# Four-layer gated cross-attention and expert block: a re-ordered first stage, its key work moved into the first expert layer, and the zero fill issued from ACT's queue

## The chip, the cores and the metric

One NeuronCore of one Trainium2 chip runs the whole program. The metric is the device time of one execution in microseconds. Each time given for a kernel as a whole is a median over several executions; the trace is of one execution, taken by the hardware profiler.

## The reference, cut to what matters

The input `x` has 8 batches of 128 tokens with 256 features; the context `ctx` has the same shape. Four layers follow one another, each one an attention-like block and an expert block, both added to `x` with a gate:

```python
x = x + tanh(g_xattn[0]) * wkv_recurrence(time_decay, time_first, layernorm(x), ctx)   # layer 0
x = x + tanh(g_ffn[0])   * top2_experts(layernorm(x))        # 8 experts of 176 + a shared one of 352
x = x + tanh(g_xattn[1]) * masked_attention(layernorm(x), ctx)                          # layer 1
x = x + tanh(g_ffn[1])   * top4_experts_with_capacity(layernorm(x))   # 32 experts of 128, 256 seats each
x = x + tanh(g_xattn[2]) * attention_32_heads_rms(layernorm(x), ctx)  # layer 2: k = rmsnorm(ctx @ Wk.T) per head of 8
x = x + tanh(g_ffn[2])   * golden_experts_with_lora(layernorm(x))     # 8 of 256; Wg, Wu, Wd of 2 experts get Ga@Gb etc.
x = x + tanh(g_xattn[3]) * int8_attention(layernorm(x), ctx)          # layer 3: wq, wp rounded to 127 steps per row
x = x + tanh(g_ffn[3])   * top_p_experts(layernorm(x))                # 8 of 512
```

The recurrence of layer 0 keeps three running values per feature (`pp`, `aa`, `bb`): with k = layernorm(x) and v = ctx, `y_t = (e1*aa + e2*v) / (e1*bb + e2)`, where e1, e2, e1b, e2b are exponentials of differences to a running maximum. The kernel computes it by scans over all tokens.

Of layers 2 and 3, some things depend on the context or the weights alone: the keys and values (`ctx @ Wk.T`, `ctx @ Wv.T`), the RMS norm of the keys of layer 2, the weight tiles of the two experts with a low-rank addition, and the rounded `wq`, `wp`. The kernel before computes all of these in its first stage.

## The kernel before, in words

The program is written engine by engine, each with its own ordered list of instructions, and the engines meet only through semaphores. An engine that waits for a semaphore holds up everything behind it in its own list; this is what sets the order of the work. `link(...)` makes an engine wait for its own last instruction. SP only issues DMAs; POOL also issues the indirect ones.

**First stage (about 0 to 119 us).** It does the recurrence of layer 0 and the context work of layers 2 and 3 side by side.

- SP (L422 to L454) loads `x` (one DMA, 1 MB), small vectors, `ctx`, the key and value weights, then `wqp3` and, four times in turn, a weight tile of layer 2 (`fold`, L440) that gets its low-rank addition and is written to DRAM (`folded`, L442). Only then come `wr`, `wq2`, `bq3`, `bp3`, `mask` and the first two weight tiles of the first expert layer (L468).
- PE transposes `ctx` (L1580), then the normalised `x` (`turn(0)`, L1367), then goes through 8 batches `b`: two products of 512 columns (L1635 for layer 2, L1640 and L1641 for layer 3), the transposes of the keys of layer 3 (`turn_k3`, L1611), and after every second `b` the low-rank products (`fold_products`, L1601). After that it turns the rounded weights (L1654, L1658), the recurrence's result (L1668) and the keys of layer 2 (`turn_k2`, L1626).
- ACT copies `ctxT` (L885) and the turned `x` (L863), then per `b` copies and splits the products (L946 to L958), copies `k3T` (L930), and before `b` = 2 and 6 runs the four exponentials of one half of the features (`wkv_exp`, L893). After the loop: a guess of the inverse root by Ln and Exp (L903, L905), the copies `wi`, `wscale`, and the split and copy of each batch of keys (`k2_hi` L916, `k2_out` L936).
- DVE normalises `x` (L2038), then in `wkv()` makes the arguments for both halves `c` (L2052 to L2060, with four minima and maxima each), rounds the weights (`weight_scales`, L2100 to L2112), and per `c` does two scans (L2066, L2068), four products and sums, a reciprocal (L2073) and a product (L2075). Then it scales half of the layer-2 keys (L2271) and adds the recurrence to `x` (`add_banks`, L2085).
- POOL per `b` sums squares for the key norm (L682 to L684) and splits the keys of layer 3 (L687), does the two products of the recurrence (`wkv`, L660), adds the low-rank part (`fold_lora`, L667), scales the diagonals (L673), refines the norms (L694 to L697) and scales and splits the other half of the keys (L703, L711).
- Before the first expert layer, DVE waits for all keys, splits the first weight tile (`gu_lo`, `down_lo`) and normalises `x` again (L2038); PE has `turn(1)` behind it.

**First expert layer, `ffn(0)` (about 119 to 254 us).** 14 tiles of 128 hidden features, each in two halves of 512 tokens. A weight is split in two half-precision parts, so each product is three. For tile `k` PE does `gate_up(k, 0)`, `down(k-1, 0)`, `gate_up(k, 1)`, `down(k-1, 1)` (12 matmuls each, L1406 and L1418). The elementwise chain of one half goes ACT `silu` (L994), DVE `gated` (L2160), POOL `weigh` (L723), ACT `h_hi` (L1020), DVE `h_lo` (L2167). The order within a tile is fixed in both lists:

```python
# ACT: down_hi(k)  silu(k,0)  gu_hi(k+1)  h_hi(k,0)  silu(k,1)  h_hi(k,1)
# DVE: down_lo(k)  gated(k,0) gu_lo(k+1)  h_lo(k,0)  gated(k,1) h_lo(k,1)
```

SP's `loads_0` issues for each tile two broadcast loads of router weights (L499), the weight load (L478) and `clear(i)` (L488): two DMAs per tile that write zeros to the DRAM tables `seats` (8192 rows of 1152 bytes, 9.4 MB) and `slots` (4096 rows of 1024 bytes, 4.2 MB), 28 DMAs in all. POOL waits for all of them (L757) before it scatters tokens into `seats`.

**Layer 1's experts.** After the router, POOL issues 32 indirect DMAs into `seats` (L761, from 304 to 346 us); PE's first transpose of an expert's rows (`expert_turn`, L1532) waits for them and for the loads behind them. DVE meanwhile prepares diagonals (L2404) and splits two weight tiles (L2420).

Of the kernel before, what the change touches and what calls it, by code (L numbers as in the profile page):

```python
# [25 lines left out]
F32 = mybir.dt.float32  # L26
# [8 lines left out]
P = 128  # L35
# [41 lines left out]
def build(nc, a, out):  # L77

    with ExitStack() as ctx:  # L79
# [64 lines left out]
        k_raw = xn  # L144
        k_norm = sb("k_norm", [P, 3, B, H2])
        k_st = sb("k_st", [P, 2, H2, 4, DH2], F16)
        k_sq = k_st[:, 0, :, :, :].rearrange("p h i d -> p (h i d)").bitcast(F32).rearrange("p (k d) -> p k d", k=2)
# [5 lines left out]
        class Arena:  # L153
# [38 lines left out]
        wk_d = ar.take([2, LW])  # L192
        wk_e = ar.take([KD, 4, LW])
        wk_ev = ar.take([2, LW])

        lora = W16[0:LORA_R, :, :, :].rearrange("p a b c -> p (a b c)").bitcast(F32)\
            .rearrange("p (k d) -> p k d", d=D)
        fold = W[:, 0, :]
        fold_add = W[:, 1, :]
        wq_s = sb("wq_s", [P, 3, 4])  # L200
        wq_f = wb[:, 0, :].rearrange("p (w o d) -> p w o d", w=2, o=KD)
        wq_i = wb[:, 1, 0:HALF].bitcast(BF16).rearrange("p (w o d) -> p w o d", w=2, o=KD)
        wq_diag = wb[:, 1, HALF:T].rearrange("p (k o) -> p k o", k=4)
# [42 lines left out]
        m_dest = ar.take([E1, CT]).bitcast(U32)  # L246
        e_x = ar.take([3, CT, ROW])
        e_xT = ar.take([2, 2, KD, CAPACITY], F16)
        e_w16 = ar.take([2, WROW], F16)
        e_y = [ar.take([CT, D]) for _ in range(3)]  # L250
        ar.at = at_back = ARENA - 4 * TOP1 * D
# [71 lines left out]
        KEYS_BEFORE = (2, 6)  # L323

        K2_ORDER = (0, 4, 1, 5, 2, 6, 3, 7)
# [38 lines left out]
        def steps_at(n):  # L364

            return range(max(n - FIRST_UNIT, 0) * 3 // 4, max(n + 1 - FIRST_UNIT, 0) * 3 // 4)

# [53 lines left out]
        def _(sp):  # L421
            sp.dma_start(x[:, :, :], a["x"].rearrange("b s d -> s b d")).then_inc(sem("x_in"), 16)  # L422
# [9 lines left out]
            sp.dma_start(wq_f, a["wqp3"]).then_inc(sem("wqp_in"), 16)  # L432
            for k in range(LORA_T):
                if k:
                    sp.wait_ge(sem("folded_out"), 16 * k)
                if k % (F2 // P) == 0:
                    if k:
                        sp.wait_ge(sem("fold_mm"), k)
                    sp.dma_start(lora[:, :, :], a["lora"][:, k * P // F2]).then_inc(sem("lora_in"), 16)
# [40 lines left out]
            def clear(i):  # L480

                if i == 0:
                    sp.wait_ge(sem("set_up"), SET_UP["zeros"])
# [52 lines left out]
            def loads_1():  # L536
                for k in range(4):
                    expert_weights(k)
# [2357 lines left out]
```

## Time and profile before

| what | value |
|---|---|
| runs without the profiler, median of 3 | 1089.8 us (1087.68 to 1095.57) |
| the profiled execution's own time | 1082.81 us |
| its span, first to last instruction | 1081.0 us |
| mean granted TensorE clock | 0.905 |
| busy share of the span: PE, DVE, ACT, POOL | 80%, 60%, 48%, 35% |

The profiled execution lies 7.0 us under the median of the runs without it. The busy share says how much of the span an engine worked; it is an average over stages with different limits, so each stage is read by itself.

### The profile page before, as it was taken

What the parts mean: (1) busy time and instruction counts of PE and PEld (TensorE: products, weight loads), DVE (VectorE), ACT (ScalarE), POOL (GpSimd) and SP (SyncE); (2) the same over time, 40 slices, a digit from 0 to 9 for tenths busy, and PEclk for the clock granted to TensorE, in tenths of its full rate; (3) what the DMA queues carried; (4) which work ended last, traced back from release to release, by engine and by line L of the source; (5) the groups of instructions that cost most, each with busy time, mean ns of one, the idle gap of its engine ahead of it and who ended that gap; (6) DMA issues with size and microseconds to landing.
All of it is one profiled execution on the core that took longest, in us unless ns stands there. A gap on an engine that the chain in (4) does not pass through costs nothing. (4 is left out here: it accounts for less than half of the span.)

```text
span 1081.0 us, 17338 instructions
## 1 busy us (share of the span) xinstructions
PE 865.8 (80%) x6353; PEld 536.8 (50%) x6353; DVE 649.7 (60%) x1383; ACT 523.8 (48%) x862; POOL 380.7 (35%) x335
## 2 busy tenths in 40 slices
PE   5875669997530777788888888778789899999997
PEld 3434436665310656656454455445445556555554
DVE  5967624446882677727435367765766666844444
ACT  3555524442210787715567844356346677433332
POOL 4977123332256355520214483200155324300000
PEclk9785589998765899989698999999899999999999
DMA  5022077781013677641203344211235453533332
GB/s 165 31 73 71 1 243 235 223 262 63 1 77 127 194 236 237 203 160 47 59 2 89 117 121 157 74 45 38 66 121 173 133 158 122 175 93 99 102 102 83
DMA packets 60430, 129.12 MB, mean 119 GB/s; under 512 B 9507, under 2 KB 25265, under 8 KB 60354
## 3 DMA queue, kind: packets, MB, share of 16 engines
q1 hardware_dynamic: 55746, 119.17, 35.6%
q0 software_dynamic: 4608, 8.94, 2.2%
q8 instruction: 47, 0.77, 0.3%
q14 instruction: 29, 0.24, 0.1%
HBM read 83.95 MB, written 48.27 MB: 122 GB/s over the span
## 5 line engine op out<-in xcount | busy, mean ns | idle before, releaser
L1463 PE MATMUL ps<-turned_buf,W 128*128 128x512 f16 x576 | 137.9, 391 | 8.3 <-POOL W L783 6.0
L2220 DVE SCALAR_TENSOR_TENSOR ctx_sb<-ps,ctx_sb 128x512 f32<-128x512 f32 x96 | 66.3, 691 | 128.6 <-PE ps L1463 87.6
L1463 PE MATMUL ps<-turned_buf,wb 128*128 128x512 f16 x576 | 135.3, 385 | 3.9 <-POOL wb L783 3.8
L780 POOL TENSOR_SCALAR W<-W 128x768 f32<-128x768 f32 x32 | 69.6, 2174 | 143.4 <-ACT wb L1063 73.9
L1051 ACT ACTIVATE ctxT<-ctx_sb 128x512 f16<-128x512 f32 x96 | 60.3, 628 | 118.7 <-DVE ctx_sb L2220 118.5
L2227 DVE TENSOR_TENSOR ctxT<-ctx_sb,ctxT 128x512 f16<-128x512 f32 x96 | 68.9, 718 | 64.1 <-ACT ctxT L1051 63.6
L1043 ACT ACTIVATE ctx_sb<-ps 128x512 f32<-128x512 f32 x96 | 57.2, 596 | 86.1 <-PE ps L1463 85.9
L1406 PE MATMUL ps<-turned_buf,W 128*128 128x512 f16 x360 | 90.4, 407 | 7.4 <-DVE W L2172 4.9
L1463 PEld LDWEIGHTS ps<-turned_buf,W 128*128 128x128 f16 x576 | 56.2, 101 | 74.4 <-issue 9.1
L1463 PEld LDWEIGHTS ps<-turned_buf,wb 128*128 128x128 f16 x576 | 55.9, 99 | 66.6 <-issue 5.5
L768 POOL DMA_INDIRECT slots<-arena x64 | 62.2, 972 | 59.9 <-ACT arena L1114 49.1
L1479 PE MATMUL ps<-W,ctxT 128*128 128x256 f16 x576 | 72.0, 276 | 6.9 <-DVE x L2236 3.6
L1479 PE MATMUL ps<-wb,ctxT 128*128 128x256 f16 x576 | 70.9, 273 | 6.3 <-DVE ctxT L2227 6.1
L723 POOL TENSOR_TENSOR arena<-arena,wb 128x512 f32<-128x512 f32 x28 | 39.0, 1393 | 96.1 <-DVE arena L2160 69.5
L1479 PEld LDWEIGHTS ps<-W,ctxT 128*128 128x128 f16 x576 | 55.3, 99 | 24.4 <-issue 10.5
L1479 PEld LDWEIGHTS ps<-wb,ctxT 128*128 128x128 f16 x576 | 55.0, 98 | 22.8 <-DVE ctxT L2227 7.6
L1406 PEld LDWEIGHTS ps<-turned_buf,W 128*128 128x128 f16 x360 | 36.9, 103 | 50.5 <-issue 18.3
L1532 PE MATMUL ps<-ident,arena 128*128 128x128 f32 x128 | 21.6, 296 | 44.1 <-DMA arena<-seats 44.0
L2167 DVE TENSOR_TENSOR arena<-arena 128x512 f16<-128x512 f32 x30 | 21.1, 704 | 56.8 <-ACT arena L1020 56.5
L642 POOL TENSOR_TENSOR rstd<-veps,mhalf 128x4 f32<-128x4 f32 x13 | 15.1, 1163 | 112.2 <-DVE veps L2026 112.1
L2236 DVE SCALAR_TENSOR_TENSOR x<-ps,arena,x 128x256 f32<-128x256 f32 x128 | 52.9, 476 | 2.5 <-PE ps L1479 2.4
L1418 PE MATMUL ps<-W,arena 128*128 128x256 f16 x360 | 45.0, 278 | 9.9 <-DVE arena L2167 9.9
(396 smaller groups left out, 1751.9 us busy)
## 6 DMA issues: line engine op xcount, KB each, us to landing
W<-in_w SPq DMA_DIRECT2D x79, 384.0 KB, 3.8
arena<-seats SPq DMA_DIRECT2D x32, 288.0 KB
kept<-W SPq DMA_DIRECT2D x24, 384.0 KB, 4.2
kept<-wb SPq DMA_DIRECT2D x24, 384.0 KB, 4.2
W<-kept SPq DMA_DIRECT2D x24, 384.0 KB, 3.0
wb<-kept SPq DMA_DIRECT2D x24, 384.0 KB, 3.1
wb<-in_w SPq DMA_DIRECT2D x16, 384.0 KB, 4.0
seats<-k_norm SPq DMA_DIRECT2D x8, 720.0 KB, 5.4
```

The costliest lines, as they stand in the source:

```text
L723: nc.gpsimd.tensor_tensor(f_h[:, half, :], f_g[:, half, :], wb[:, k % 2, half * HALF:(half + 1) * HALF], ALU.mult).then_inc(sem("h_full"), 1)
L768: nc.gpsimd.indirect_dma_start(slots, bass.IndirectOffsetOnAxis(ap=m_dest[:, k, c:c + 1], axis=0), e_y[k % 3][:, c, :], None, bounds_check ...
L780: link(nc.gpsimd.tensor_scalar(W[:, n % 2, :], W[:, n % 2, :], WSCALE, None, ALU.mult))
L1043: nc.scalar.activation(h_s[:, g % 2, :], bank(4), ACT.Silu, scale=1.0 / WSCALE).then_inc(sem("silu_done"), 1)
L1051: nc.scalar.activation(h_16[:, g % 2, 0, :], h_g[:, g % 2, :], ACT.Copy).then_inc(sem("h_hi"), 1)
L1406: last = nc.tensor.matmul(bank(2 * g + half), W16[:, k % 2, w, g * D + c * P:g * D + (c + 1) * P], x16[:, i, c, half * HALF:(half + 1) * H ...
L1418: last = nc.tensor.matmul(ps[:, 4 + t // 2, (t % 2) * D:(t % 2 + 1) * D], f_h16[:, k % 2, i, t * S:(t + 1) * S], W16[:, k % 2, w, 2 * D:3 ...
L1463: last = nc.tensor.matmul(bank(4 + n), w4[k % 4][:, w, n * D + c * P:n * D + (c + 1) * P], x16[:, i, c, half * HALF:(half + 1) * HALF], st ...
L1479: last = nc.tensor.matmul(ps[:, 6 + t // 2, (t % 2) * D:(t % 2 + 1) * D], h_16[:, g % 2, i, t * S:(t + 1) * S], w4[k % 4][:, w, 2 * D:3 * ...
L2220: nc.vector.scalar_tensor_tensor(h_g[:, g % 2, :], bank(5), 1.0 / WSCALE, h_s[:, g % 2, :], ALU.mult, ALU.mult).then_inc(sem("gated"), 1)
L2227: nc.vector.tensor_tensor(h_16[:, g % 2, 1, :], h_g[:, g % 2, :], h_16[:, g % 2, 0, :], ALU.subtract)\
L2236: ins = nc.vector.scalar_tensor_tensor(x[:, t, :], ps[:, 6 + t % 4 // 2, (t % 2) * D:(t % 2 + 1) * D], l_w[:, L - 2, t, e:e + 1], x[:, t, ...
```

## The change

In words, by engine:

- **Loads.** `x` comes in two halves. The weight tiles 0 and 1 of the first expert layer, `wr`, `bq3`, `bp3` and `mask` are issued right behind the key weights. `wqp3`, the low-rank factors and the layer-2 tiles are loaded later, in a new `for_later()` behind `wkv_y` 2 (the recurrence's end), into the arena.
- **Recurrence.** PE turns `x` before `ctx`. DVE's eight minima and maxima go; ACT makes them with Relu and takes one exponential over two rows (`wkv_exp(c, k)`, called after `b` = 0, 1, 2, 3). POOL's products are `wkv(c, k)`, before `keys(b)` of `b` = 1, 2, 4, 5. PE turns the result of half `c` after `b` = 5 and 6.
- **Keys of layer 2.** In the first stage only the raw keys are copied. Squares, norms, scaling and splitting become `k2_work(k)` on DVE and `k2_hi` on ACT, called after tiles `k` = 0 to 12 of `ffn(0)`; the transposes and `k2_out` come ahead of layer 1's experts.
- **Rounded weights.** `weight_scales()` runs on DVE after tile 2, `scale_diagonals()` on ACT after tile 2, the transposes `whole_weights()` ahead of the experts.
- **Low-rank tiles.** `fold_products` on PE between the key transposes, `fold_sum` on DVE behind the diagonals.
- **Loops.** `ffn(0)`'s loops on ACT and DVE are written out, those of PE and POOL stay.
- **Zero fill.** `clear(i)` goes. ACT issues 12 DMAs (8 for `seats`, 4 for `slots`, 1024 rows each) after the copies of `x` and `ctx` and ahead of its loop over `b`.

The core of the diff:

```diff
@@ SP @@
-            sp.dma_start(x[:, :, :], a["x"].rearrange("b s d -> s b d")).then_inc(sem("x_in"), 16)
+            for h in range(2):
+                sl = slice(4 * h, 4 * h + 4)
+                sp.dma_start(x[:, sl, :], a["x"].rearrange("b s d -> s b d")[:, sl, :]).then_inc(sem("x_in", h), 16)
...
+            for i in range(2):
+                sp.dma_start(W[:, i, :], a["w0"][i]).then_inc(sem("w_in", i), 16)
...
-            def clear(i):
...
+            def for_later():
+
+                sp.wait_ge(sem("wkv_y"), 2)
+                sp.dma_start(wq_f, a["wqp3"]).then_inc(sem("wqp_in"), 16)
+                for e in range(LORA_E):
+                    sp.dma_start(lora[e * LORA_R:(e + 1) * LORA_R, :, :], a["lora"][:, e]).then_inc(sem("lora_in"), 16)
+                for k in range(2):
+                    sp.dma_start(fold[:, k, :], a["w2"][k]).then_inc(sem("fold_in", k), 16)
+
+            def fold_back(k):
+
+                sp.wait_ge(sem("fold_sum"), k + 1)
+                sp.dma_start(folded[k], fold[:, k % 2, :]).then_inc(sem("folded_out"), 16)
+                if k + 2 < LORA_T:
+                    sp.wait_ge(sem("folded_out"), 16 * (k + 1))
+                    sp.dma_start(fold[:, k % 2, :], a["w2"][k + 2]).then_inc(sem("fold_in", k % 2), 16)
@@ ACT @@
+            def wkv_exp(c, k):
+
+                n = 2 * c + k + 1
+                act.wait_ge(sem("wkv_arg"), n)
+                for e, sign in ((2 * k, -1.0), (2 * k + 1, 1.0)):
+                    ins = nc.scalar.activation(wk_e[:, c, e, :], wk_d[c][:, k, :], ACT.Relu, scale=sign)
+                ins.then_inc(sem("wkv_relu"), 1)
+                act.wait_ge(sem("wkv_relu"), n)
+                nc.scalar.activation(wk_e[:, c, 2 * k:2 * k + 2, :], wk_e[:, c, 2 * k:2 * k + 2, :], ACT.Exp, scale=-1.0)\
+                    .then_inc(sem("wkv_exp"), 1)
+
+            act.wait_ge(sem("set_up"), SET_UP["zeros"])
+            for rows, wide, pieces in ((seats, ROW, 8), (slots, D, 4)):
+                j = rows.shape[0] // P
+                for i in range(pieces):
+                    lo, hi = j * i // pieces, j * (i + 1) // pieces
+                    act.dma_start(rows.rearrange("(j p) d -> p j d", p=P)[:, lo:hi, :],
+                                  no_rows[:, 0:wide].unsqueeze(1).to_broadcast((P, hi - lo, wide))).then_inc(sem("seats_zero"), 16)
...
+            def k2_hi(b):
+
+                act.wait_ge(sem("k2_norm"), b + 1)
+                nc.scalar.activation(k2_parts(b)[:, :, 0:4:2, :], k_scr[:, b % 2, :].rearrange("p (h d) -> p h d", d=DH2)
+                                     .unsqueeze(2).to_broadcast((P, H2, 2, DH2)), ACT.Copy).then_inc(sem("k2_hi"), 1)
...
+                for k in range(NT[L]):
+                    tile(L, k, meanwhile=wT_copy if k == 0 else None)
+                    if 4 <= k < 4 + B:
+                        k2_hi(k - 4)
+                    if k == 2:
+                        scale_diagonals()
@@ POOL @@
             inv_sqrt(0)
-            for b in range(B):
-                if b in KEYS_BEFORE:
-                    wkv(KEYS_BEFORE.index(b))
+            for b in range(B - 1):
+                if b in EV_AT:
+                    wkv(*EXPS_AT[EV_AT.index(b)])
                 keys(b)
...
+            keys(B - 1)
             inv_sqrt(1)
             weigh_hidden()
@@ PE @@
             for b in range(B):
...
                 if b >= 1:
                     turn_k3(b - 1)
-                if b % 2:
-                    fold_products(b // 2)
+                if b in WKV_TURN_AT:
+                    turn_wkv(WKV_TURN_AT.index(b))
...
             shared()
+            for b in range(B):
+                turn_k2(b)
+                if b % 2:
+                    fold_products(b // 2)
             turn_over()
+            whole_weights()
             experts()
@@ DVE @@
+            def k2_work(k):
+
+                if k in (0, 1):
+                    k2_squares(2 * k)
+                    k2_squares(2 * k + 1)
+                if k == 2:
+                    k2_guess()
+                    k2_refine()
+                if k == 3:
+                    k2_refine()
+                    k2_refine()
+                if 5 <= k < 5 + B:
+                    k2_lo(k - 5)
+                if 4 <= k < 4 + B:
+                    k2_normed(k - 4)
...
+                for k in range(NT[L]):
                     tile(L, k)
+                    k2_work(k)
+                    if k == 2:
+                        weight_scales()
```

In `k2_work`, `k2_squares` is a product and a reduction over 512 columns, `k2_guess` two and `k2_refine` three instructions over 256 columns, all linked; `k2_normed` is a product over 256 columns and `k2_lo` a difference over 512, which waits for `k2_hi` of its batch.

## Rows read from the trace of the kernel before

**Rows 1.** Busy time by stretch of the span; the last is one key batch.

```profile
core 0: us, PE busy (x) PEld busy (x) DVE busy (x) ACT busy (x) POOL busy (x), PEclk, DMA share, GB/s
0.00:119.20 119.20, 77.71 (x312) 45.43 (x312) 86.01 (x118) 59.75 (x124) 85.07 (x101) 0.77 0.25 77
119.20:159.20 40.00, 29.14 (x159) 15.30 (x160) 17.66 (x36) 11.15 (x21) 5.01 (x4) 0.72 0.45 140
159.20:254.20 95.00, 93.47 (x587) 57.06 (x584) 45.24 (x74) 39.31 (x72) 33.94 (x24) 1.00 0.71 227
53.00:58.45 5.45, 5.45 (x20) 2.25 (x20) 5.38 (x4) 2.92 (x9) 5.37 (x5) 1.00 0.00 0
```

**Rows 2.** Timeline of DVE, first stage: start, us, engine, line, operation.

```profile
18.19 0.76 DVE L2052 TENSOR_SCALAR arena<-turned_buf,wdec 128x1032 f32<-128x1032 f32 x1 [5.17 <-ACT turned_buf L863]
40.26 1.22 DVE L2100 TENSOR_REDUCE wq_s<-wb 128x4 f32<-128x1024 f32 x1
46.04 2.30 DVE L2066 TENSOR_TENSOR_SCAN arena<-arena 128x1032 f32<-128x1032 f32 x1
56.29 6.60 DVE L2073 RECIPROCAL arena<-arena 128x1032 f32<-128x1032 f32 x1
72.35 3.20 DVE L2066 TENSOR_TENSOR_SCAN arena<-arena 128x1032 f32<-128x1032 f32 x1 [8.02 <-ACT arena L893]
119.23 2.67 DVE L2038 TENSOR_SCALAR xn<-x,mv,rstd 128x256 f32<-128x256 f32 x8
```

**Rows 3.** Timeline of PE and ACT, first stage.

```profile
11.01 3.65 PE L1580 MATMUL ps<-ident,ctx_sb 128*128 128x128 f32 x16 [11.01 <-DMA ctx_sb<-in_ctx]
30.47 3.97 ACT L893 ACTIVATE arena<-arena 128x1032 f32<-128x1032 f32 x4
```

**Rows 4.** DMA issues of SP: one issue, then min/median/max ns by line.

```profile
0.72 0.44 SPq L422 DMA_DIRECT2D x<-in_x  x1
...
L488 SPq DMA_DIRECT2D seats<-k_norm x14: 413/586/591, 139.0 to 237.0; - x14
L488 SPq DMA_DIRECT2D slots<-k_norm x14: 501/526/607, 139.7 to 237.6; - x14
...
L478 SPq DMA_DIRECT2D W<-in_w x12: 762/1393/1592, 143.8 to 230.6; - x12
L513 SPq DMA_DIRECT2D W<-in_w x16: 328/580/582, 245.6 to 448.0; - x16
```

**Rows 5.** Timeline of ACT and DVE, one tile of the first expert layer.

```profile
190.35 0.60 ACT L994 ACTIVATE arena<-ps 128x512 f32<-128x512 f32 x1 [0.34 <-PE ps L1406]
197.04 0.63 ACT L1020 ACTIVATE arena<-arena 128x512 f16<-128x512 f32 x1 [2.27 <-POOL arena L723]
198.07 0.60 ACT L994 ACTIVATE arena<-ps 128x512 f32<-128x512 f32 x1
197.71 0.69 DVE L2167 TENSOR_TENSOR arena<-arena 128x512 f16<-128x512 f32 x1 [2.12 <-ACT arena L1020]
198.70 0.69 DVE L2160 SCALAR_TENSOR_TENSOR arena<-ps,arena 128x512 f32<-128x512 f32 x1
```

**Rows 6.** Waits from 160 to 250 us: us in total, times, longest.

```profile
ACT arena L994 <- PE ps L1406: 2.8, 11, 0.3
```

**Rows 7.** Operations like those that move: min/median/max ns.

```profile
L1183 ACT ACTIVATE arena<-arena x8: 613/626/669, 491.9 to 534.2; 128x512 f16<-128x512 f32 x8
L2526 DVE TENSOR_TENSOR arena<-arena x8: 681/693/694, 492.6 to 534.9; 128x512 f16<-128x512 f32 x8
L2271 DVE TENSOR_TENSOR xn<-xn,k_norm x4: 420/638/853, 98.7 to 100.2; 128x256 f32<-128x256 f32 x4
```

**Rows 8.** ACT's wait for a weight tile early in the first expert layer.

```profile
152.34 0.63 ACT L1001 ACTIVATE W<-W 128x512 f16<-128x512 f32 x1 [5.45 <-DMA W<-in_w]
```

**Rows 9.** Timeline ahead of layer 1's experts: DVE, then PE.

```profile
329.18 0.94 DVE L2420 SCALAR_TENSOR_TENSOR arena<-wb,arena 128x768 f16<-128x768 f32 x1
...
350.40 2.00 PE L1532 MATMUL ps<-ident,arena 128*128 128x128 f32 x8 [26.82 <-DMA arena<-seats]
```

More of the change, by code:

```diff
@@ L538, in loads_1 @@
                     expert_weights(k)
+                for k in range(LORA_T):
+                    fold_back(k)
                 sp.wait_ge(sem("seated"), 16 * B * TOP1)
@@ L577, in _ @@
             loads_1()
+            sp.wait_ge(sem("folded_out"), 16 * LORA_T)
             head_loads(2)
@@ L1138, in ffn @@
             def ffn(L):
-                for k in range(G[L]):
-                    tile(L, k, meanwhile=wT_copy if L == 0 and k == 0 else None)
-                with act.Fori(0, TURNS[L]) as j:
-                    for k in range(G[L], 2 * G[L]):
-                        tile(L, k, j)
-                for k in range(G[L] * (1 + TURNS[L]), NT[L]):
-                    tile(L, k, last=(k == NT[L] - 1))
-            act.wait_ge(sem("late_in"), 16 * 5)
+                for k in range(NT[L]):
[4 more added lines that the diff above has]
+                        scale_diagonals()
+            act.wait_ge(sem("late_in"), 16 * 4)
             nc.scalar.activation(wr16[:, 0, :, :], wr[:, :, :], ACT.Copy).then_inc(sem("wr_hi"), 1)
@@ L1526, in expert_turn @@
                 if k < 2:
-                    pe.wait_ge(sem("gated"), EXPERT)
+                    pe.wait_ge(sem("fold_sum"), LORA_T)
                 else:
@@ L1670, in _, with whole_weights @@
-            last.then_inc(sem("wkv_turn"), 1)
-            for n in range(B):
-                turn_k2(n)
-            pe.wait_ge(sem("k2_ready"), B)
+            def whole_weights():
+                pe.wait_ge(sem("wq_step"), 2)
+                for w in range(2):
+                    for c in range(KD):
+                        for o in range(KD):
+                            k = (w * KD + c) * D + o * P
+                            last = nc.tensor.transpose(ps[:, 4, :].bitcast(BF16)[:, k:k + P], wq_i[:, w, o, c * P:(c + 1) * P],
+                                                       identb[:, :])
+                last.then_inc(sem("wi_turn"), 1)
+                pe.wait_ge(sem("wq_diag"), 1)
+                for k in range(4):
+                    last = nc.tensor.matmul(ps[:, 5, k * P:(k + 1) * P], ones[:, :], wq_diag[:, k, :], start=True, stop=True)
+                last.then_inc(sem("wscale_mm"), 1)
@@ L1703, in _ @@
             shared()
+            for b in range(B):
+                turn_k2(b)
+                if b % 2:
+                    fold_products(b // 2)
             turn_over()
+            whole_weights()
             experts()
@@ new lines, in k2_lo @@
+            def k2_lo(b):
+                dve.wait_ge(sem("k2_norm"), b + 1)
+                dve.wait_ge(sem("k2_hi"), b + 1)
+                parts = k2_parts(b)
+                nc.vector.tensor_tensor(parts[:, :, 1:4:2, :], k_scr[:, b % 2, :].rearrange("p (h d) -> p h d", d=DH2)
+                                        .unsqueeze(2).to_broadcast((P, H2, 2, DH2)), parts[:, :, 0:4:2, :], ALU.subtract)\
+                    .then_inc(sem("k2_split"), 1)
+            def k2_work(k):
[12 more added lines that the diff above has]
+                    k2_normed(k - 4)
@@ L2405, in _ @@
             ins.then_inc(sem("back_diag"), 1)
+            for k in range(LORA_T):
+                fold_sum(k)
             def expert_x(k):
```

353 lines of the change are left out of this document (122 added, 231 removed).

## The prediction

> **What bounds the kernel now.** I read first the busy time by stretch [rows 1], since the shares over the whole span hide two stages of different kind. From 0 to 119.2 us no engine is full: DVE works 86.0 us, POOL 85.1, PE 77.7, ACT 59.8. A stage in which nobody is full and nobody is idle is bound by a chain, so I read the timelines of DVE and ACT next [rows 2, 3]. DVE starts the recurrence at 18.19, waiting for the copy of the turned `x`; it does the weight scales (from 40.26) before its first scan (46.04); the second half's first scan (72.35) waits 8.02 us for exponentials that stand behind ACT's batch 5; the second normalisation starts only at 119.23, after the keys of layer 2. From 159.2 to 254.2 PE is busy 93.5 of 95.0 us at a granted clock of 1.00, the 2.4 GHz level, and DVE only 45.2, ACT 39.3: by that row DVE and ACT have half of their time to give away. The third view says otherwise. In one tile [rows 5] ACT's `silu` comes at 190.35 and the next tile's at 198.07: 7.7 us, in which ACT, DVE and POOL hand two halves to each other with no gap of more than 0.3 us between an end and the next start. In the waits of this stage [rows 6] ACT's `silu` waits for PE 2.8 us in all, 0.3 at most. PE's tile takes 7.8 us (95.0 us for about 12.2 tiles), the elementwise chain 7.7: two loops of one length. DVE's idle time lies inside this chain, not beside it.
>
> **Part 1: the first stage.** I follow the new chain that ends last. C stands for the time in which ACT issues the 12 zero-fill DMAs.
> - `x` in halves lets statistics start about 1.5 us earlier (an estimate: they wait for half of the bytes, and the second half's no longer follow late), and turning `x` before `ctx` takes the 3.65 us of context transposes [rows 3] out of the way: the recurrence starts at 18.19 - 1.5 - 3.65, about 12.9 [rows 2]. ACT has copied `x` and `ctx` at about 16.5.
> - From 16.5 + C on, ACT goes through the batches. One costs ACT 2.92 us (the last row of [rows 1]; the square that goes is 0.3 of it, hand-overs make up for it), the first 2.0. One `wkv_exp` costs two Relu and an exponential over 2064 columns, by 3.97 us for four of 1032 [rows 3] about 4.1 with its wait. Two batches and two calls: 2.0 + 4.1 + 2.9 + 4.1 = 13.1. DVE's arguments (5.9 us a half) are long done.
> - DVE then: two products 2.4, two sums 2.5, reciprocal 6.6, product and gaps 1.9 (the reciprocal from [rows 2], the others lie between 1.2 and 1.7 each): 13.4. The second half adds two scans of 2.3 and the same 13.1: 17.7. `wkv_y` 2 comes at 16.5 + C + 13.1 + 13.4 + 17.7 = 60.7 + C.
> - Behind it stands batch 7, whose products PE does only after turning the recurrence: turning 2, products with a slow start 6.7, `turn_k3` 0.6, ACT 0.8, POOL's split (`keys(7)`, which also stands ahead of `inv_sqrt(1)`) 1.3, `turn_k3` 0.6, copy 1.0, the weight's high parts 1.3, low parts 1.1, hand-overs 0.3: 15.7. DVE's adding and statistics (two of 3.5 us) lie beside it. The normalisation starts at 76.4 + C instead of 119.2: a gain of 42.8 - C. I take 2 off for POOL and DVE slowing each other (the first scan took 2.30 at 46.04 and 3.20 at 72.35 [rows 2]).
>
> What C is, the trace does not show, since nothing here issues 13.6 MB at once. Below: 12 at the 0.44 us of the 1 MB load of `x` or the 0.41 to 0.61 of a `clear`, 5.3 us [rows 4]. Above: ACT is held until nearly all has drained; at the rate of 227 GB/s at a DMA share of 0.71 [rows 1], 320 GB/s full, 13.6 MB take 43 us. Between: a weight load behind two fill DMAs took 1.39 us to issue, where the same load without them took 0.58 [rows 4], so a queue with about 1000 rows ahead already holds its issuer. Two at 0.5 and ten at 1.39 make 15 us. I take C = 15, the row nearest to a train of such DMAs. Gain: 42.8 - 15 - 2 = 26 us.
>
> One rule weighs on this. In the trace, two fill DMAs cost SP 1.1 us and the load behind them 0.8 more [rows 4]. The Trainium skill (DMA: Bandwidth & Descriptors, "Issuing engines are not separate DMA queues") says that issuing from several engines only saves the sequencer's time to start a DMA, which is usually small beside the DMA itself. By that rule C is the lower end; it is the first rival below.
>
> **Part 2: the first expert layer.** The 28 fill DMAs go from SP. Early on, ACT waited 5.45 us for tile 2's weights [rows 8], behind the fill DMAs of tiles 0 and 1; that wait goes. PE's loop gains nothing, it was full. What comes in are instructions behind `h_lo(k, 1)` on DVE and behind `h_hi(k, 1)` on ACT, ahead of the next tile. DVE ends `h_lo` at 198.40 and starts the next `gated` at 198.70, with `down_lo` between [rows 5]: there is no gap to put them in, each lengthens the loop.
> - Tiles 0 and 1: two squares and two reductions of 0.7, linked: 2.9 us each. They eat the 5.45 us that the weight wait gave: 0.
> - Tile 2: guess and refinement 2.1 (five linked instructions of 0.3 to 0.45), weight scales up to `wq_i` 5.2 (from 40.26 to the scan at 46.04 it took 5.8 with the rest [rows 2]), then ACT's four diagonals 1.0, which ACT waits for: `silu` comes at the end of `h_lo` + 8.4 + 0.4 of `down_hi`, `gated` 9.1 later than now.
> - Tile 3: six linked instructions, 2.9.
> - Tiles 4 to 11: DVE `k2_lo` 0.69 (from tile 5), `k2_normed` 0.42, then ACT `k2_hi` 0.63 [rows 7], and ACT waits for DVE. `k2_hi` ends 1.11 + 0.1 + 0.63 behind the end of `h_lo`, which is itself 0.73 behind the end of `h_hi` (198.40 - 197.67 [rows 5]): 2.55 longer, in tile 4 1.9. Sum 1.9 + 7 x 2.55 = 19.8.
> - Tile 12: 0.7.
> Together 32.5; the chain had 0.1 a tile to spare and about 1.5 at the start: 30 us longer. From below: if the two loops had the 3 us of lead that a half's `h_lo` has on its `down` anew in every tile, only tile 2 would show, and with its own lead taken off it costs 6 to 10. From above: if PE also falls to the lower of its two clock levels in the gaps, one cold `gate_up` in tile 3, 33.
>
> **Part 3: the rest.** The eight key transposes and copies, low-rank sums, `whole_weights`: DVE ends its last split at 330.1, PE gets the first expert's rows at 350.4 [rows 9], 20 us later, behind the indirect DMAs. `fold_sum` 0 starts at 328.2, where the two splits of 0.94 start now; sum 1.1, tile out and next tile in 7, sum 2 at 337.5, out and in of the other buffer, sum 3 at 341; then the over-transposes and `whole_weights` to about 344. All is hidden with 6 us left; without that cover it costs what exceeds it. The zero fill is over by 70 us, far ahead of POOL's wait. The later loads of `wqp3` and the low-rank tiles start at 76 and are needed at about tile 2. Writing out the loops: 0, since the loops show no gap.
>
> **Sum.** -26 + 30 + 0 = +4 us. The profiled execution's own time was 1082.8 (span 1081.0), so 1086.8; the median of the runs shown stands 7.0 above it, so I predict 1094 us. About 1%, 11 us, is what a measurement of this kernel can tell from no change.
>
> **The rivals.**
> - *Issuing is cheap (C = 5.3).* For it: every fill issue took 0.6 us at most, and the 1 MB of `x` 0.44 [rows 4]. Against: the 1.39 us [rows 4]. Gain 35.5, loss 30: -5.5, so 1084. Chance 0.25.
> - *ACT is held by its own queue (C = 43).* The place is ACT between its copies and batch 0; PE stands behind it with the second batch's product, DVE with the first scan. It decides from C = 21 on, where the sum passes 1%: 42.8 - 21 - 2 = 20 against 30. For it: 1.39 us behind only 1 MB; 12 pieces are 13 times as much. Against: among 12 such weight loads the longest was held 1.59 us, never for a whole drain. Gain about 0, loss 30: 1120. Chance 0.25.
> - *The moved key work hides in DVE's half-idle time.* For it: DVE 45.2 of 95.0 us [rows 1], and `h_lo` comes some 3 us ahead of its `down`. Against: rows 5 and 6. Then the loss is about 8: -26 + 8 = -18, so 1072. Chance 0.15.
>
> **How the numbers follow.** Forecast 0.35, rivals 0.25, 0.25, 0.15. The range reaches from the third rival to the second, 1072 to 1122; the forecast's own case is 1083 to 1106 (C from 8 to 25, the expert layer from 26 to 34). Faster by over 1% (below 1079): the third rival 0.14, a part of the first 0.07, together 0.21. Slower by over 1% (above 1101): the second rival 0.25 and a third of the forecast's case 0.11, 0.36. Within 1%: 0.43.
>
> **What would show it.** In the changed kernel's trace: the recurrence's first instruction on DVE at 13; ACT's first key copy at 16.5 + C, which reads C off directly; the second normalisation at 76 + C; then the time from that to the end of `ffn(0)`, 135 us now (119.2 to 254.2), at 165, with tiles 4 to 11 at 10.3 us each, PE's clock still at its upper level, and tile 2's at about 17; PE's first `expert_turn` waiting for the seats' DMA, not for DVE. Wrong would be tiles of 7.8 us with key work in them, a C under 8 or over 25, or a start of the experts that waits for `fold_sum`.

## The result

| | before | after |
|---|---|---|
| median of 4 runs, beside each other | 1091.8 us (1087.7 to 1095.6) | 1120.4 us (1117.2 to 1126.1) |
| ratio | | 1.0275, 95% interval 1.0228 to 1.0321 |
| the profiled execution: own time, span | 1082.8, 1081.0 | 1126.1, 1124.2 |

The change makes the kernel 2.7% slower. The forecast was 1094 us; the measured time is that of the second rival (1120), but the profile reaches it by another road than that rival's. The two profiled spans differ by 43.2 us and the medians by 28.6: the profiled execution of the kernel before (1082.8) lies below all four of its runs here. So a part of the first number is not the program's, and the experiments had to separate it.

I cut both spans at the same events: the second normalisation, the end of `ffn(0)`, POOL's first scatter, PE's first transpose of an expert's rows, the end. Busy time by stretch, after the change:

```profile
core 0: us, PE busy (x) PEld busy (x) DVE busy (x) ACT busy (x) POOL busy (x), PEclk, DMA share, GB/s
0.00:110.10 110.10, 57.29 (x192) 28.35 (x192) 68.45 (x87) 43.71 (x82) 36.01 (x45) 0.78 0.52 174
110.10:268.00 157.90, 125.58 (x744) 71.79 (x744) 84.05 (x155) 54.03 (x104) 38.62 (x28) 0.92 0.32 93
268.00:318.50 50.50, 29.20 (x171) 20.07 (x168) 41.05 (x138) 11.08 (x17) 10.00 (x16) 0.76 0.04 14
318.50:379.20 60.70, 25.58 (x152) 20.06 (x152) 28.80 (x85) 13.40 (x17) 32.14 (x32) 0.56 0.35 127
379.20:1124.20 745.00, 639.05 (x5097) 398.74 (x5097) 436.42 (x943) 398.14 (x623) 213.73 (x158) 0.95 0.37 117
```

The same stretches before, from the second on (the first is in [rows 1]):

```profile
119.20:254.20 135.00, 122.62 (x744) 72.36 (x744) 62.89 (x110) 50.46 (x92) 38.95 (x28) 0.92 0.63 201
254.20:304.10 49.90, 27.45 (x170) 19.92 (x168) 41.01 (x137) 11.06 (x17) 10.01 (x16) 0.74 0.04 14
304.10:350.40 46.30, 5.92 (x32) 3.95 (x32) 24.34 (x77) 3.95 (x7) 32.73 (x32) 0.54 0.30 113
350.40:1081.00 730.60, 632.08 (x5097) 395.14 (x5097) 435.43 (x943) 398.57 (x623) 213.92 (x158) 0.96 0.39 119
```

The second column is the length: 119.2 to 110.1 (-9.1), 135.0 to 157.9 (+22.9), 49.9 to 50.5 (+0.6), 46.3 to 60.7 (+14.4), 730.6 to 745.0 (+14.4). The first two were forecast with other sizes, the last two as zero. In the fourth, DVE and ACT have more to do than before (28.8 and 13.4 us) and yet more than half of the stretch free: somebody waits.

**First stage.** ACT's timeline: the fill's DMA issues (ACTq), then the first key copy.

```profile
15.21 0.39 ACTq L854 DMA_DIRECT2D seats<-k_st  x1
15.62 0.59 ACTq L854 DMA_DIRECT2D seats<-k_st  x1
16.25 17.06 ACTq L854 DMA_DIRECT2D seats<-k_st  x6
33.34 12.38 ACTq L854 DMA_DIRECT2D slots<-k_st  x4
45.77 0.38 ACT L875 ACTIVATE k2T<-ps 128x256 f32<-128x256 f32 x1 [29.38 <-issue]
```

The first two DMAs take 0.39 and 0.59 us, the next ten 29.4 together, 2.9 each; the key copy waits for them alone ("issue" in the brackets: the profile shows nothing that it waited for). So C, the time in which ACT is held, is 29.4, where 15 was taken and 43 was the upper bound. Behind it stands DVE's first scan:

```profile
14.00 0.76 DVE L1992 TENSOR_SCALAR arena<-turned_buf,wdec 128x1032 f32<-128x1032 f32 x1 [2.39 <-ACT turned_buf L811]
...
51.48 4.15 DVE L2005 TENSOR_TENSOR_SCAN arena<-arena 128x1032 f32<-128x1032 f32 x1 [26.02 <-ACT arena L845]
...
110.14 2.67 DVE L1978 TENSOR_SCALAR xn<-x,mv,rstd 128x256 f32<-128x256 f32 x8
```

DVE starts the recurrence at 14.00 (18.19 in [rows 2], 12.9 forecast) and is idle for 26.0 us before the scan.

**First expert layer.** One tile with key work, ACT first, then DVE:

```profile
202.94 0.58 ACT L925 ACTIVATE arena<-ps 128x512 f32<-128x512 f32 x1
...
209.33 0.63 ACT L951 ACTIVATE arena<-arena 128x512 f16<-128x512 f32 x1 [2.22 <-POOL arena L679]
211.66 0.63 ACT L870 ACTIVATE k2T<-k_st 128x512 f16<-128x512 f32 x1 [1.69 <-DVE k_st L2076]
...
212.50 0.58 ACT L925 ACTIVATE arena<-ps 128x512 f32<-128x512 f32 x1
...
206.66 0.69 DVE L2158 TENSOR_TENSOR arena<-arena 128x512 f16<-128x512 f32 x1 [1.82 <-ACT arena L951]
...
210.00 0.69 DVE L2158 TENSOR_TENSOR arena<-arena 128x512 f16<-128x512 f32 x1 [2.04 <-ACT arena L951]
210.60 0.68 DVE L2085 TENSOR_TENSOR k2T<-k_st,k2T 128x512 f16<-128x512 f32 x1
211.21 0.42 DVE L2076 TENSOR_TENSOR k_st<-k2T,k_norm 128x256 f32<-128x256 f32 x1
```

`silu` to `silu` takes 9.56 us (202.94 to 212.50), 7.72 in [rows 5]. ACT's `h_hi` ends at 209.96; DVE's `h_lo`, `k2_lo` and `k2_normed` follow, then ACT's `k2_hi` at 211.66, all as forecast. What the forecast read past stands in brackets: DVE waited 2.04 us for ACT in front of the second `h_lo`, and 1.82 in front of the first.

**Ahead of the experts.** POOL scatters from 318.5 to 360.1. Meanwhile ACT, DVE and PE:

```profile
331.77 1.02 ACT L864 ACTIVATE k2T<-ps 128x1024 f16<-128x1024 f16 x1 [4.70 <-remote]
360.69 1.02 ACT L864 ACTIVATE k2T<-ps 128x1024 f16<-128x1024 f16 x1 [27.90 <-issue]
...
343.11 0.50 DVE L2381 TENSOR_SCALAR ctxT<-ident,arena 128x128 f32<-128x128 f32 x2 [0.85 <-issue]
344.53 0.29 DVE L2381 TENSOR_SCALAR ctxT<-ident,arena 128x128 f32<-128x128 f32 x1 [0.93 <-issue]
...
345.94 0.42 DVE L2207 TENSOR_TENSOR arena<-ps,arena 128x256 f32<-128x256 f32 x1
...
354.42 2.08 PE L1539 MATMUL ps<-arena 64*128 64x128 f32 x8 [20.47 <-remote]
```

PE has turned the third batch of keys at 328.3; ACT copies it at 360.69, 0.6 us behind POOL's last scatter, after 27.9 us in which it waited for nothing that the profile shows. ("remote" in the brackets: a semaphore event came last that the profile gives to no instruction of the core.) DVE's diagonals follow one another without a wait in the program, and have gaps of 0.9 us. DVE ends the first low-rank sum at 346.4, and PE's product that waits for it starts 8 us later ("remote"). The experts start 19 us behind the last scatter, 4 us before the change.

### The profile page after: what moved, and what is told of

Read it like the earlier page. It is cut to its first block and busy times, and to the rows that moved or that the text cites. A ratio compares the mean times of both kernels' runs of the same rounds, so it can differ in the third digit from the quotient of the medians.

```text
span 1124.2 us, 17139 instructions
## 1 busy us (share of the span) xinstructions
PE 876.7 (78%) x6353; PEld 539.0 (48%) x6353; DVE 658.8 (59%) x1406; ACT 520.4 (46%) x842; POOL 330.5 (29%) x279
## 3 DMA queue, kind: packets, MB, share of 16 engines
q10 hardware_dynamic: 12480, 13.63, 3.5%
## 5 line engine op out<-in xcount | busy, mean ns | idle before, releaser
L2217 DVE SCALAR_TENSOR_TENSOR ctx_sb<-ps,ctx_sb 128x512 f32<-128x512 f32 x96 | 66.3, 691 | 130.4 <-PE ps L1399 89.0
L1342 PE MATMUL ps<-turned_buf,W 128*128 128x512 f16 x360 | 91.3, 410 | 25.8 <-DVE W L2163 23.4
L1415 PEld LDWEIGHTS ps<-wb,ctxT 128*128 128x128 f16 x576 | 55.0, 98 | 22.9 <-DVE ctxT L2224 7.6
L951 ACT ACTIVATE arena<-arena 128x512 f16<-128x512 f32 x30 | 18.9, 629 | 80.1 <-POOL arena L679 72.6
L1354 PE MATMUL ps<-W,arena 128*128 128x256 f16 x360 | 47.0, 284 | 11.4 <-DVE arena L2158 11.4
L1354 PEld LDWEIGHTS ps<-W,arena 128*128 128x128 f16 x360 | 36.2, 102 | 23.5 <-issue 14.2
```

What stands on the lines that cost most here:

```text
L1342: last = nc.tensor.matmul(bank(2 * g + half), W16[:, k % 2, w, g * D + c * P:g * D + (c + 1) * P], x16[:, i, c, half * HALF:(half + 1) * H ...
L1354: last = nc.tensor.matmul(ps[:, 4 + t // 2, (t % 2) * D:(t % 2 + 1) * D], f_h16[:, k % 2, i, t * S:(t + 1) * S], W16[:, k % 2, w, 2 * D:3 ...
L1415: last = nc.tensor.matmul(ps[:, 6 + t // 2, (t % 2) * D:(t % 2 + 1) * D], h_16[:, g % 2, i, t * S:(t + 1) * S], w4[k % 4][:, w, 2 * D:3 * ...
L2217: nc.vector.scalar_tensor_tensor(h_g[:, g % 2, :], bank(5), 1.0 / WSCALE, h_s[:, g % 2, :], ALU.mult, ALU.mult).then_inc(sem("gated"), 1)
```

## The experiments

Three sets and a last single kernel (set 4) ran, each set on one chip with the kernel before beside it, four chips in all. The kernel before took 1091.1 and 1091.8 us in sets 1 and 2, and 1082.6 and 1083.7 in sets 3 and 4. Times are compared within a set, and between sets 1 and 2, whose kernels before lie 0.7 us apart; otherwise only ratios are.

| kernel | built on | median us | ratio to before, 95% | set |
|---|---|---|---|---|
| again | the change | 1119.0 | 1.0241 (1.0203 to 1.0278) | 1 |
| fill_from_sp | the change | 1093.8 | 1.0017 (0.9995 to 1.0040) | 1 |
| fill_spread | the change | 1095.1 | 1.0044 (1.0016 to 1.0072) | 1 |
| keys_later | the change | 1113.6 | 1.0222 (1.0175 to 1.0270) | 1 |
| keys_in_gaps | fill_from_sp | 1078.6 | 0.9873 (0.9807 to 0.9939) | 2 |
| all_in_gaps | keys_in_gaps | 1064.5 | 0.9739 (0.9676 to 0.9803) | 2 |
| scatter_waits | fill_from_sp | 1120.1 | 1.0253 (1.0177 to 1.0329) | 2 |
| turned_early | fill_from_sp | 1089.3 | 0.9973 (0.9939 to 1.0007) | 2 |
| fill_wide | the change | 1093.9 | 1.0101 (1.0066 to 1.0135) | 3 |
| combined | all_in_gaps + turned_early | 1045.6 | 0.9664 (0.9605 to 0.9723) | 3 |
| best | combined | 1041.2 | 0.9610 (0.9574 to 0.9647) | 3 |
| third_look | the change | 1096.5 | 1.0133 (1.0099 to 1.0168) | 4 |

### again and third_look: what belongs to the program

No edit in either.

> The changed kernel once more, nothing edited. It asks which parts of the 43 us between the two profiled spans (1081.0 and 1124.2) come back in a second profile. If they belong to the kernel: second normalisation at 110, end of the first expert layer at 268, ACT idle for 28 us before its third key copy (332.8 to 360.7) and the experts' start at 379, experts' loop 117 us long, span 1124. If a part is chance of one execution: the stall before the third key copy is gone or elsewhere, the start of the experts moves to 365 (last scatter plus 5 us), and the experts' loop is 106 to 112 us, as in the kernel before (105).

In again the normalisation stands at 110.5, the end of the layer at 269.1, ACT's third key copy at 360.25 after 28.1 us, the experts' start at 380.1, 19 us behind the last scatter. It all comes back, the stall at the same instruction. The experts' loop (first transpose to last) took 113 us, 116 in the profile of the change and 105 in that of the kernel before.

> The changed kernel once more, unedited. In the last set of kernels (fill_wide, combined, best) the kernel before took 1082.6 us, where it took 1091 to 1092 beside the others, and no engine was late during the scatter; turned_early and combined have the same instructions there, the first with stalls, the second without. Theory (the stall belongs to the conditions of a set, not to the program; it comes with slower experts' loops): if the kernel before takes 1080 to 1085 here, the changed kernel has no stall, the experts start 5 us behind the last scatter, its time is 1082.6 - 9.1 + 23 = 1097 us, ratio 1.013; if the kernel before takes 1089 to 1093, the stall of 28 us on ACT is there again and the ratio is 1.024 to 1.028. Rival (the written-out layout or the moved work removed it in the last set): the stall is there whatever the kernel before takes.

Here the kernel before took 1083.7 us, the changed one 1096.5. ACT's key copies:

```profile
324.90 1.94 ACT L864 ACTIVATE k2T<-ps 128x1024 f16<-128x1024 f16 x2 [5.08 <-PE ps L1561]
327.42 1.94 ACT L864 ACTIVATE k2T<-ps 128x1024 f16<-128x1024 f16 x2 [0.58 <-PE ps L1561]
346.68 1.94 ACT L864 ACTIVATE k2T<-ps 128x1024 f16<-128x1024 f16 x2 [17.32 <-PE ps L1561]
```

The first four copies run in two pairs; the 17.3 us before the next are PE's wait for the first low-rank sum behind DVE's diagonals, the program's own order. The last scatter ends at 360.0, the experts start at 364.3, and the stretch from the first scatter to there is as long as before the change (46.3):

```profile
317.70:364.30 46.60, 23.88 (x153) 19.04 (x153) 28.18 (x85) 13.03 (x17) 32.87 (x32) 0.61 0.45 164
```

Against the profile of the kernel before the stretches are -8.7, +21.9, +0.4, +0.3 and -2.5: +11.4 us of span. So the program accounts for 13 us (1.3%) on this chip, and the 14 us ahead of the experts belong to the chip or its condition; with them the ratio is 1.024 to 1.028. An edit as the cause of their absence is out, since nothing was edited. The longer experts' loop goes with the sets too, but not with the stall: it takes 108 to 119 us in every profile of sets 1 and 2, 112 even in scatter_waits, which has no stall, and 104 to 107 in sets 3 and 4. The kernel before was profiled once, at 1082.8 us; how it spends its 8 us more in sets 1 and 2 is not shown.

### fill_from_sp and fill_spread: the size of C

```diff
             act.wait_ge(sem("set_up"), SET_UP["zeros"])
-            for rows, wide, pieces in ((seats, ROW, 8), (slots, D, 4)):
...
-                    act.dma_start(rows.rearrange("(j p) d -> p j d", p=P)[:, lo:hi, :],
...
             for b in range(B):
...
+                for n in range(ZERO_PIECES * b // B, ZERO_PIECES * (b + 1) // B):
+                    clear(n)
```

This is fill_spread (`clear(n)` issues piece n); in fill_from_sp the whole loop stands in SP's list behind the load of `mask`.

> Only the issuer of the 12 fill DMAs changes, from ACT to SP, behind SP's first loads. Theory (ACT is held by its own queue, 29.4 us): ACT's first key copy at 17 instead of 45.8, second normalisation at 110.1 - 29.4 = 81, all later stages shifted as a block, time 1120.4 - 28 = 1092 us. SP is held instead, for 25 to 30 us, and nobody waits for it. Rival (the 13.6 MB slow the stage through the DMA engines, whoever issues them: key weights and context arrive late): first key copy still after 35, normalisation above 100, time above 1110 us.

> ACT still issues all 12 fill DMAs, but one or two at the end of each batch's copies instead of in one train. Theory A (a DMA is cheap to issue while at most two of this size are queued, and ACT is held only for what the queue has not yet drained): batches are about 3 us long and a piece drains in 3 to 3.5 us, so each of the 12 pieces costs 0.5 to 2 us: 6 to 20 us in all instead of 29.4, normalisation at 87 to 100, time 1096 to 1111 us. Theory B (each of these DMAs costs its issuer about 3 us whenever it is issued, for the making of its descriptors): still 12 times 2.5 to 3, the hold is only cut into pieces, time 1115 to 1122 us.

SP's fill issues in fill_from_sp, then ACT's first key copy:

```profile
9.94 21.98 SPq L449 DMA_DIRECT2D seats<-k_st  x8
31.96 13.22 SPq L449 DMA_DIRECT2D slots<-k_st  x4
...
18.23 0.39 ACT L876 ACTIVATE k2T<-ps 128x256 f32<-128x256 f32 x1 [2.13 <-PE ps L1578]
```

Now SP is held, for 35 us where 25 to 30 were expected, and nobody waits for it. The normalisation starts 26.5 us earlier, and the time falls by 25 us:

```profile
83.65 2.67 DVE L1979 TENSOR_SCALAR xn<-x,mv,rstd 128x256 f32<-128x256 f32 x8
```

In fill_spread each of the 12 issues takes 0.37 to 0.61 us, while ACT's copies run on:

```profile
27.12 0.37 ACTq L856 DMA_DIRECT2D seats<-k_st  x1
27.18 0.39 ACT L884 ACTIVATE k_raw<-ps 128x256 f32<-128x256 f32 x1
27.51 0.61 ACTq L856 DMA_DIRECT2D seats<-k_st  x1
```

The normalisation starts at 83.62. So a DMA of 1.1 MB has no price of its own near 3 us (theory B), and the 13.6 MB don't slow the stage from beside (the rival). What costs is a third such DMA behind two that have not drained. It came out just below the cheap end of the expectation (1095.1 us for 1096, the normalisation at 83.6 for 87), since the 5 us or more between two visits let a pair drain.

### fill_wide: what fills the queue

```diff
-                j = rows.shape[0] // P
+                flat = rows.rearrange("(p j) d -> p (j d)", p=P).rearrange("p (j w) -> p j w", w=2 * D)
+                j = flat.shape[1]
```

> The changed kernel with its train of 12 fill DMAs on ACT, the same bytes, but written as rows of 2048 bytes instead of 1152 and 1024, so about 6,700 packets instead of 12,480. It asks what fills the queue. Theory A (bytes: ACT is held until the train has drained, and the drain runs at the 320 GB/s of the memory side): the hold stays at 26 to 30 us, time 1117 to 1121 us. Theory B (packets or descriptors: the queue holds about two DMAs' worth of them, some 2,000, and they drain at a fixed rate): now four DMAs fit and the rest drains in half the time or a little more, hold 12 to 18 us, time 1105 to 1110 us.

```profile
16.33 13.81 ACTq L855 DMA_DIRECT2D seats<-k_st  x6
30.16 12.16 ACTq L855 DMA_DIRECT2D slots<-k_st  x4
42.37 0.38 ACT L876 ACTIVATE k2T<-ps 128x256 f32<-128x256 f32 x1 [25.84 <-issue]
```

The hold is 25.8 us, at the lower end of theory A, for the drain: from 20 us until the hold is nearly over (42 here, 44 in the changed kernel) the DMA engines move 379 GB/s here and 376 in the changed kernel, where the expectation took 320. So 6,848 packets in place of 12,480 drain hardly faster. What stands in the queue when ACT comes free is less clear: 2,561 packets and 2.6 MB in the changed kernel, 1,901 and 3.8 MB here, counted from the queue's packets after that moment. Neither bytes nor packets alone set it. The ratio, 1.010 to third_look's 1.013, agrees with 3.6 us saved, but the two intervals overlap.

### keys_later, keys_in_gaps, all_in_gaps: where the work hides

keys_later takes `k2_normed`, `k2_hi` and `k2_lo` out of the tiles 4 to 12 and puts them behind DVE's diagonals.

> The scaling and splitting of the layer-2 keys (k2_normed, k2_hi, k2_lo, 8 batches) leaves the tiles 4 to 12 of the first expert layer and stands where POOL scatters the seats, between DVE's diagonals and the experts. Fill from ACT as in the changed kernel. Theory (two loops of one length: each tile with key work is 1.9 us longer, 9.6 for 7.7): tiles 4 to 11 back at 7.7, from the normalisation to the end of the layer 158 - 15 = 143 us, and the work hides in the 40 us of the scatter: time 1120.4 - 15 = 1105 us. Rival (it only moves the wait: keys, copies, low-rank sums form a chain behind the diagonals at 345): layer 15 us shorter, but the experts start 8 to 15 us later than the last scatter plus 5, time 1113 to 1122 us.

The layer's stretch is 17.6 us shorter (140.3), the experts start 30 us behind the last scatter for 19, and the time falls by 5 us: the rival holds here, the work went into a wait. But the stall was there too: in front of its first low-rank sum DVE stood 17.4 us, from 330.5 to 347.9 ("remote"), so how much of the work would hide without the stall is not shown. The next two leave it in its tile and move it by a few instructions; in program order, tile k:

```diff
   DVE: down_lo(k), gated(k, 0), gu_lo(k + 1)
+  DVE: k2_normed(k - 4)
   DVE: h_lo(k, 0), gated(k, 1)
+  DVE: k2_lo(k - 5)
   DVE: h_lo(k, 1)
-  DVE: k2_lo(k - 5), k2_normed(k - 4)
   ACT: h_hi(k, 0), silu(k, 1)
+  ACT: k2_hi(k - 4)
   ACT: h_hi(k, 1)
-  ACT: k2_hi(k - 4)
```

> Built on fill_from_sp. The same instructions in the same tiles (4 to 12) of the first expert layer, but each inside a gap of its engine instead of behind the last instruction of the tile: DVE's k2_normed behind gu_lo (the trace shows 1.8 us idle there), k2_lo behind the second gated (2.0 idle), ACT's k2_hi behind the second silu (2.2 idle). Theory (the chain ACT, POOL, DVE is full, but each engine is idle in it while another one works): tiles back from 9.6 to 7.7 us, 8 x 1.9 = 15 us less, time 1093.8 - 15 = 1079 us. Rival (the prediction's view: no engine has room, wherever it is put, or the extra semaphore steps and the port shared with POOL eat it): tiles stay above 9.2, time above 1090 us.

> As keys_in_gaps, and the rest of the moved work too: the squares of tiles 0 and 1, guess and refinements of tiles 2 and 3, the rounding of the weights cut into four parts over tiles 4 to 7, ACT's four diagonals into tile 12. Theory: nothing of the moved work is left on the chain, so another 2.9 + 2.9 + 9 to 12 (tile 2) + 2.9 less what starts late, together 12 to 16 us below keys_in_gaps: 1063 to 1067 us, and the stretch from the second normalisation to the end of the layer 133 to 137 us, as in the kernel before (135). Rival: the linked pairs (1.4 us and two semaphore steps) don't fit into gaps of 1.8, tiles 0 to 3 stay over 8.5 us and only 6 us come back: 1073 us.

A tile of all_in_gaps on DVE (left out: `down_lo`, the first `gated`):

```profile
175.27 0.68 DVE L2157 SCALAR_TENSOR_TENSOR W<-W 128x512 f16<-128x512 f32 x1
175.87 1.49 DVE L2086 TENSOR_TENSOR k_st<-k2T,k_norm 128x256 f32<-128x256 f32 x1
177.78 0.69 DVE L2152 TENSOR_TENSOR arena<-arena 128x512 f16<-128x512 f32 x1 [0.42 <-ACT arena L952]
178.39 0.68 DVE L2145 SCALAR_TENSOR_TENSOR arena<-ps,arena 128x512 f32<-128x512 f32 x1
178.99 0.68 DVE L2095 TENSOR_TENSOR k2T<-k_st,k2T 128x512 f16<-128x512 f32 x1
```

`k2_normed` takes 1.49 us here, 0.42 behind the tile, while POOL's product runs beside it (175.44 to 177.09); the gap of 1.82 shrinks to 0.42 and still holds it. keys_in_gaps measured 1078.6 for 1079 expected, with its tiles 5 to 11 at 7.8 us; all_in_gaps 1064.5 for 1063 to 1067. Its stretch from the normalisation to the end of the layer is 130.4 us, shorter than before the change (135.0), with all of the moved work in it and without the wait of [rows 8].

### scatter_waits and turned_early: the late start

```diff
             pool.wait_ge(sem("seat"), 2)
+            pool.wait_ge(sem("k2_ready"), B)
+            pool.wait_ge(sem("fold_sum"), LORA_T)
```

> Built on fill_from_sp. POOL begins the 32 scatter DMAs only when all key copies and low-rank sums are done, so this work runs with POOL silent. A measurement, not an improvement. Theory (while POOL issues scatters, the other engines' instructions and semaphores arrive late, up to 28 us): with POOL silent the key transposes and copies follow one another without the gap of 28 us, low-rank sum 0 at the end of the diagonals, PE's next product within 0.3 us of it, and the last sum is over about 15 us after the diagonals (three more sums and two round trips of a tile through DRAM). Rival (the gaps are waits of the program itself: bank, buffer or tile not ready): the same gaps of 20 to 28 us between the second and the third key copy with POOL silent. In both cases the scatter starts only then, and the time is 1105 to 1125 us.

```profile
299.75 1.94 ACT L867 ACTIVATE k2T<-ps 128x1024 f16<-128x1024 f16 x2 [5.17 <-PE ps L1564]
302.27 1.94 ACT L867 ACTIVATE k2T<-ps 128x1024 f16<-128x1024 f16 x2 [0.58 <-PE ps L1564]
321.02 1.94 ACT L867 ACTIVATE k2T<-ps 128x1024 f16<-128x1024 f16 x2 [16.81 <-PE ps L1564]
```

With POOL silent the copies run in pairs, the diagonals have no gap, PE's product starts 0.06 us behind the first sum, and the last sum ends 14.4 us behind the diagonals. On the same chip the kernels whose copies ran beside the scatter (keys_in_gaps, all_in_gaps) started their experts 18.5 and 18.6 us behind the last scatter. So in these runs the stall needs the scatter; third_look shows that the scatter is not enough.

> Built on fill_from_sp. The eight key transposes and their copies go ahead of the scatter (three behind the attention of layer 1, five behind the shared expert's first products, banks 6 and 7), the low-rank sums use two pairs of banks and stand ahead of DVE's diagonals. Theory (the experts start 19 us behind the last scatter because key copies and sums are caught in the scatter): now only the sums are in it, early; the experts start 5 us behind the last scatter as in the kernel before, 14 us earlier: 1093.8 - 14 = 1080 us. Rival 1: sums 2 and 3 are still caught, gain 0 to 5 us, 1089 to 1094. Rival 2: the transposes delay the router or the shared expert, and the scatter starts later by as much as is won.

The transposes were over before the scatter, but DVE's list was caught instead: from 14 us into the scatter on, its instructions came up to 7.8 us late, and its last weight split ended 54.5 us behind the first scatter (345.9); in combined, without the stall, the same list ends 37.6 us behind it. The experts start 9 us behind the last scatter. 4.5 us were won of 14 (0.9973 against fill_from_sp's 1.0017, intervals that overlap), as rival 1 has it.

### combined and best

> all_in_gaps and turned_early in one kernel: fill from SP, key work and rounding in the gaps, key transposes and the first two low-rank sums ahead of or at the start of the scatter. If the two gains add: 1064.5 - 4.5 = 1060 us. If the experts' start is bound by DVE's chain through the scatter in both: no better than all_in_gaps, 1064.

> combined, and four moves that take work off DVE while POOL scatters and off the ends of two stages: the 32 diagonals go from the scatter into experts 4 to 19 (two each), the weight splits of the first two experts stand ahead of the scatter's slow part, the seat numbers go between the shared expert's two gate_up halves (the scatter starts 2 us earlier), and batch 7's products go ahead of turning the recurrence (DVE's idle 5.2 us before the first weight split goes). Theory (the experts start late because DVE's list runs on through the scatter, not because of the transposes): experts start 5 to 6 us behind the last scatter, 4 us earlier than in combined, plus 2, plus 5: 1060 - 11 = 1049 us. Rival: the diagonals cost the experts' loop what they gave (32 x 0.2 = 6.4 us), or the low-rank sums 2 and 3 still end last: 1055 to 1060 us.

No engine was late in this set: combined has turned_early's instructions at the scatter and starts its experts 4.3 us behind it. So whether the two gains add can't be said from 0.966 against all_in_gaps' 0.974, which holds the chip's share. best is 4.4 us below combined on the same chip, for 11 expected, and the intervals of the two overlap. Its normalisation starts at 79.2 (83.35 in combined), its scatter 48.6 us behind the end of the layer (50.0); the 4 us of the experts' start had nothing to win here. It is 3.9% faster than the kernel before, and the fastest of the study.

## Why the prediction was right or wrong

The range of 1072 to 1122 held, and in part by luck. It reached up to 1122 for the second rival's sake, which has the whole loss in C and the layer; measured were a smaller C, a smaller loss in the layer, and on top a stall that no rival had. The program alone, 1.3% slower in third_look, lies inside the range too, 10 us above the forecast, in the part beyond 1% to which the prediction gave 0.36.

In the profiled execution the forecast of 1086.8 missed by 39.3 us: 16.9 from the first stage, -7.1 from the first expert layer, 0.6 up to the scatter, 14.4 ahead of the experts, 14.4 behind.

- **The step that failed: "two at 0.5 and ten at 1.39 make 15 us".** The two cost 0.98, the ten 29.4. The 1.39 us were a weight load behind two fill DMAs of 1 MB together: the row showed that a filling queue holds its issuer, and I took it for the price of one issue. The price is the drain of what lies ahead. The upper bound was built that way and left out what may stay queued: 13.6 MB less 2.6, at 376 GB/s, make 29.3 us. The second rival had mechanism and place right, and its deciding point of 21 us was passed, as was the prediction's own sign of being wrong, a C over 25. The Trainium skill's rule (DMA: Bandwidth & Descriptors, "Issuing engines are not separate DMA queues"), that the time to start a DMA is usually small beside the DMA itself, agrees with the first two (0.39 and 0.59 us) and with all twelve of fill_spread (0.61 at most); the ten at 2.9 are its exception.
- **The rest of the first stage: 2 us off.** 76.4 + 29.4 + 2 = 107.8 for 110.1. Without the hold it is 5 off: 78.4 for 83.65, since DVE was done at 77.0 and waited 5.2 us for ACT, and ACT 10.1 for batch 7's products, which PE does behind the turning of the recurrence. best moved them ahead and won 4.1.
- **First expert layer: mechanism right, 30 for 22.9.** Each of the tiles 5 to 11 was priced 2.55 longer and is 1.8: from the end of `h_hi` to the next `silu` it takes 2.54 for 0.40, 2.14 more, and 0.3 came back inside the tile. The forecast added full durations, and in the trace an instruction starts up to 0.1 us before the one ahead of it has ended. That is 5 of the 7 us. Tiles 0 and 1, forecast as unchanged, came out 3.1 shorter. Tile 2 took 18.8 us (17 forecast). Tile 3 took 7.2 (10.6 forecast), because the refinements on DVE did not hold ACT's next `silu`; they hold the `gated` behind it, and tile 4 took 11.9 (9.6 forecast). PE's granted clock over the stretch is 0.92, as before.
- **"There is no gap to put them in": true of the place, not of the engine.** [rows 5] has the 2.12 us in front of `h_lo`. The third rival fell as the change is written, and all_in_gaps shows that the room was there.
- **The rest, zero: right of the program.** In third_look the last of sums, key copies and whole weights ends at 359.4, 5 us before the experts start, for the 6 of the prediction. In the execution measured the cover was gone. Before the change DVE's list ended 26 us into the scatter, and PE and ACT had one short group each beside it; that trace, at 1082.8 us, shows none of them late, so no row of it could tell of the stall.
- **The sum.** Of the program alone -9.1 + 22.9 + 0.6 on 1082.8 make 1097; third_look measured 1096.5. Against the forecast of 1086.8 that is 10 us, in which the error of 17 in the first stage is partly hidden by that of 7 in the layer. With C at 29.4 and all else as forecast, the prediction would have been 1108.

## What to carry to other kernels

Issue a train of large DMAs from an engine with nothing behind it, or in ones and twos between its work: here issuing was nearly free for the first two, and then cost the drain. Where two loops are equally long, look at each engine's idle time inside the loop, and put moved work in front of an instruction that waits, not behind the last one. Profile both kernels beside each other before a per cent is laid on the code: here the share of the chip or its condition was as large as the program's.

## What the runs showed that was not expected

- Beside POOL's 32 scatter DMAs, on two chips, other engines were late without a wait of their own. ACT's third key copy came after 27.9, 28.1, 29.4 and 31.5 us (the changed kernel, again, fill_from_sp, fill_spread), and after 27.9 and 28.6 in keys_in_gaps and all_in_gaps, at most 4.2 us behind the last scatter; DVE's increments reached PE 6 to 9 us late. It began about 9 us after the first scatter on ACT and 24 on DVE (14 in turned_early). It was absent on two other chips (fill_wide, combined and best; third_look), and with POOL silent. What the engines share there was not tried and stays open, and so does what tells the chips apart.
- DVE's product of 256 columns took 0.42 us alone and 1.49 beside a POOL product (all_in_gaps), its scan of 1032 columns 2.31 with POOL idle (at 14.94 us of the changed kernel) and 4.15 beside a POOL product (at 51.48).
